# Causal attention over 23-step sequences: one sequence per 32 rows instead of four sequences in 92

## What is computed

```python
qk   = einsum('bthd,bshd->bhts', q, k) / sqrt(128)      # 8 heads of k and v, 2 of q on each, d = 128
gate = logG[:, :, :, None] - logG[:, :, None, :]         # logG: running sum over time of log_sigmoid(6.9 + x Wg)
a    = where(causal, qk ** 2 * exp(gate), 0)
norm = sum(a, axis=-1) + 1e-06
y    = einsum('bhts,bshd->bthd', a, v) / norm
out  = y @ Wc + bc
```

## Time and profile before

| | |
|---|---|
| median of 3 runs | 1438.3 us (1438.11 to 1441.32) |
| the profiled execution's own time | 1435.07 us |
| its span (first to last instruction) | 1433.3 us |
| TensorE busy | 1279.8 us, 89% of the span |
| VectorE busy | 915.9 us, 64% |
| ScalarE busy | 639.1 us, 45% |
| mean granted TensorE clock | 0.94 of 2.4 GHz |
| the first attention's loop | from about 140 us to about 651 us |

### The profile page before, as it was taken

The page is one execution under the profiler, slowest core; times in us unless marked ns, Lnnn a source line. Parts: engine busy times, 40 slices in busy tenths (PEclk is TensorE's granted clock), DMA queues, the critical chain, the costliest instruction groups (busy, mean ns, idle before and its releaser), DMA issues.

```text
span 1433.3 us, 28634 instructions
## 1 busy us (share of the span) xinstructions
PE 1279.8 (89%) x9689; PEld 789.5 (55%) x9690; DVE 915.9 (64%) x1920; ACT 639.1 (45%) x1086; POOL 231.4 (16%) x280
## 2 busy tenths in 40 slices
PE   6999999999999999996789999999986787859997
PEld 2447667677676767664435444544533565424443
DVE  5993665656656665668864555445348676778886
ACT  3444444554444445542325444444532433246664
POOL 2220000000000000000013333333347610110000
PEclk9997999999999999995799999999997787889999
DMA  5211452433435352422325867876336620000000
GB/s 191 73 66 62 161 199 104 182 135 143 182 141 199 123 191 103 176 89 83 141 75 200 280 220 246 318 256 208 109 121 137 100 36 2 1 0 16 22 22 26
DMA packets 42699, 184.21 MB, mean 129 GB/s; under 512 B 8688, under 2 KB 9200, under 8 KB 34832
## 3 DMA queue, kind: packets, MB, share of 16 engines
q0 software_dynamic: 19744, 95.41, 20.1%
q1 hardware_dynamic: 19440, 75.41, 14.8%
q10 hardware_dynamic: 3456, 12.58, 2.5%
HBM read 135.65 MB, written 47.73 MB: 128 GB/s over the span
## 4 chain that ended last, share of the span: by engine, by line
PE 58%; DVE 19%; issue 11%; DMA 4%; POOL 3%; ACT 2%; DVEq 1%; SPq 0%; ACTq 0%; POOLq 0%
PE ps L915 14%; PE ps L917 14%; PE ps L916 14%; PE ps L1021 3%; PE ps L1000 3%; DMA wide<-wsp 2%; DVE ff L2022 2%; DVE amf L2029 1%; PE ps L1105 1%; PE ps L1037 1%; POOL h L519 1%; PE ps L1358 1%; DVE bst L1460 1%; PE ps L1340 1%; DVE wa_lo L1387 1%
## 5 line engine op out<-in xcount | busy, mean ns | idle before, releaser
L915 PE MATMUL ps<-nT_hi,wa_hi 128*128 128x368 f16 x576 | 189.5, 329 | 11.1 <-DVE wa_lo L1387 8.1
L916 PE MATMUL ps<-nT_lo,wa_hi 128*128 128x368 f16 x576 | 189.1, 328 | 0.0
L917 PE MATMUL ps<-nT_hi,wa_lo 128*128 128x368 f16 x576 | 188.7, 328 | 0.0
L661 ACT ACTIVATE qk<-ps 128x368 f32<-128x368 f32 x128 | 60.4, 477 | 130.6 <-PE ps L917 130.5
L1751 DVE SCALAR_TENSOR_TENSOR nrm<-ps,xg,nrm 128x256 f32<-128x256 f32 x61 | 29.5, 484 | 123.8 <-ACT nrm L729 108.4
L915 PE MATMUL ps<-wide,xT 128*128 x244 | 92.7, 380 | 15.5 <-issue 12.3
L503 POOL DMA_INDIRECT xg<-xrow,idx x61 | 61.3, 1005 | 265.2 <-PE ps L1105 123.5
L1579 DVE TENSOR_TENSOR a<-sq,E 92x368 f32<-92x368 f32 x64 | 32.7, 538 | 107.1 <-ACT sq L677 107.1
L1553 DVE SCALAR_TENSOR_TENSOR wide<-ps,wide 128x368 f32<-128x368 f32 x128 | 69.3, 542 | 49.0 <-PE ps L917 49.0
L916 PE MATMUL ps<-wide,xT 128*128 x244 | 92.5, 379 | 0.0
L917 PE MATMUL ps<-wide,xT 128*128 x244 | 92.5, 379 | 0.0
(11 more groups left out here) (312 smaller groups left out, 3098.3 us busy)
## 6 DMA issues: line engine op xcount, KB each, us to landing
we_st<-in_we POOLq DMA_DIRECT2D x16, 1536.0 KB, 6.7
wsp<-we_sp POOLq DMA_DIRECT2D x16, 1536.0 KB, 5.3
wide<-wsp SPq DMA_DIRECT2D x16, 1536.0 KB, 7.6
yslot<-yt POOLq DMA_DIRECT2D x61, 256.0 KB, 4.3
wq_st<-in_ffq SPq DMA_DIRECT2D x24, 512.0 KB, 4.2
wq_st<-in_ffq ACTq DMA_DIRECT2D x24, 512.0 KB, 3.6
wide<-in_wa SPq DMA_DIRECT2D x10, 1024.0 KB, 6.1
xt<-in_x SPq DMA_DIRECT2D x12, 512.0 KB, 3.4
```

Source lines behind the costliest of these rows:

```text
L661: nc.scalar.activation(B["qk"][:, j, :], ps[:, j % 2, 0:CW], ACT.Copy, scale=(AS if j == 3 else 1.0) / WS).then_inc(b_ev, 1)
L915: nc.tensor.matmul(dst, lhs[0], rhs[0], start=start, stop=False)
L916: nc.tensor.matmul(dst, lhs[0], rhs[1], start=False, stop=False)
L917: return nc.tensor.matmul(dst, lhs[1], rhs[0], start=False, stop=stop)
```

## The change

In the first attention a sequence takes 32 rows (23 used), and four sequences stand side by side in the 128 rows. k and v are evicted into padded tiles `kp`, `vp` (16 sequences x 32 columns a chunk). The scores are 16 matmuls of 32 keys by 2 x 23 columns, each on its own 32 output partitions, and hold no products between sequences: 184 columns a chunk in place of 736. Gates and their exp have 92 columns in place of 368. The norm comes from a matmul with a block matrix of ones `blk` on the weights (one float32 matmul of 184 columns, signalled by `b_sm`), VectorE takes its reciprocal and scales the weights. The weights by values are 16 matmuls with v as the stationary side (32 rows, 128 columns) and 46 moving columns; their result is already turned, so L1037's transposes and the normalization behind them are gone. Row 23 of each 32 carries the 1e-6 (`eps_row`). `out_proj(g-1, c-1)` is placed in two halves around the sum's matmul, and `accumulate` of block 1 stands behind the scaling on VectorE. ScalarE's `unit_a_hi` moves ahead of the |w| sums in chunk 3. `gr` is read by four DMAs a head of 23 partitions x 368 values each; `lgd` is written in 92-byte pieces.

In the second attention `returned(3)`, `total_stats(3)` stand behind the first two `low`; `returned(5)`, `total_stats(5)`, `deviations` stand behind the first two rotations; the low halves of tiles 3 to 5 stand ahead of `centred(0)`; GpSimd's `turned_root(1)` stands ahead of a memset and three shares.

```diff
+        def windows(y, x):
+
+            return y[:].rearrange("p r t -> p (r t)").rearrange("p (n q s) -> p q n s", q=4, s=SL)[:, 2 * x:2 * x + 2]
+
+        def weighted(x):
+
+            return ps[:, 2 + 2 * x:4 + 2 * x, 0:REP * AT].rearrange("p q (n s) -> p q n s", s=SL)
...
-            sp.dma_start(B["gr"][0:AT], lgd[0:1, :].broadcast_to([AT, T])).then_inc(gr_in, 16)
-            sp.wait_ge(gr_in, 16)
+
+            def gates_spread(head):
+                for q in range(4):
+                    sp.dma_start(B["gr"][32 * q:32 * q + SL].rearrange("p a s -> p (a s)"),
+                                 lgd[q].rearrange("(h a) s -> h (a s)", h=HEADS)[head, :].broadcast_to([SL, AT * 4])).then_inc(gr_in, 16)
+
+            gates_spread(slice(0, 1))
+            sp.wait_ge(gr_in, 64)
...
             shares(2, 1)
+            turned_root(1)
             pool.wait_ge(wa_lo, UNITS)
             nc.gpsimd.memset(st_a[:], 0.0).then_inc(f_pad, 1)
             shares(2, 2)
-            turned_root(1)
             shares(2, 3)
...
-                nc.scalar.activation(B["qk"][:, j, :], ps[:, j % 2, 0:CW], ACT.Copy,
-                                     scale=(AS if j == 3 else 1.0) / WS).then_inc(b_ev, 1)
+                if j < REP:
+                    nc.scalar.activation(B["q"][:, j, :], ps[:, j % 2, 0:CW], ACT.Copy, scale=1.0 / WS).then_inc(b_ev, 1)
+                else:
+                    nc.scalar.activation(B["kp" if j == 2 else "vp"][:, :, 0:SL], ps[:, j % 2, 0:CW].rearrange("p (w s) -> p w s", s=SL),
+                                         ACT.Copy, scale=(AS if j == 3 else 1.0) / WS).then_inc(b_ev, 1)
 
...
                 for c in range(CH):
                     g = CH * i + c
                     for j in range(1 if c == 1 else 0, 4):
                         head_moved(g, c, j)
                     act.wait_ge(b_g, g + 1)
-                    nc.scalar.activation(B["E"][0:AT], B["gt"][0:AT], ACT.Exp).then_inc(b_E, 1)
-                    for j in range(2):
-                        act.wait_ge(b_sc, 3 * g + j + 1)
-                        nc.scalar.activation(B["sq"][0:AT, j].rearrange("p a r t -> p (a r t)"), ps[0:AT, 2 + j, 0:2 * REP * AT],
-                                             ACT.Square, scale=float(DH) ** -0.5).then_inc(b_sq, 1)
-                    act.wait_ge(b_sc, 3 * g + 3)
-                    nc.scalar.activation(B["v1"][0:AT, :, 0:DH],
-                                         ps[0:AT, 1, :].rearrange("p (a b) -> p a b", a=4), ACT.Copy).then_inc(b_ev, 1)
+                    nc.scalar.activation(B["E"][:], B["gt"][:].rearrange("p a s -> p (a s)"), ACT.Exp).then_inc(b_E, 1)
+                    act.wait_ge(b_sc, 2 * g + 1)
+                    nc.scalar.activation(B["sq"][:].rearrange("p r x -> p (r x)"), ps[:, 2, REP * AT:2 * REP * AT],
+                                         ACT.Square, scale=float(DH) ** -0.5).then_inc(b_sq, 1)
+                    act.wait_ge(b_sc, 2 * g + 2)
+                    nc.scalar.activation(B["v1"][:].rearrange("p a d -> p (a d)"), ps[:, 1, :], ACT.Copy).then_inc(b_ev, 1)
+                    if c == CH - 1:
+                        unit_a_hi(i + 1, b_pj, 4 * CH * (i + 1))
...
                     if c in (1, 3):
                         expert_hi(2 * i + c // 2)
                     if c == 0:
                         head_moved(g + 1, 1, 0)
-                    for j in range(2):
-                        act.wait_ge(b_yt, 2 * g + j + 1)
-                        nc.scalar.activation(oh[:, :, j * 2 * AT:(j + 1) * 2 * AT],
-                                             ps[:, 2 + j, 0:CW].rearrange("p (r t) -> p r t", r=REP), ACT.Copy).then_inc(b_hi, 1)
+                    act.wait_ge(b_av, g + 1)
+                    for x in range(2):
+                        nc.scalar.activation(windows(B["yT_hi"], x), weighted(x), ACT.Copy).then_inc(b_hi, 1)
...
-                        pe.wait_ge(b_lo, free(2 * g + j))
-                        for a in range(2):
-                            tok = slice((2 * j + a) * AT, (2 * j + a + 1) * AT)
-                            ins = nc.tensor.matmul(ps[0:AT, 2 + j, a * REP * AT:(a + 1) * REP * AT],
-                                                   B["qk"][:, 2, tok], B["qk"][:, 0:2, tok], start=True, stop=True)
-                        ins.then_inc(b_sc, 1)
+                    pe.wait_ge(b_lo, free(2 * g + 1))
+                    for a in range(4):
+                        for q in range(4):
+                            n = 4 * a + q
+                            out = ps[32 * q:32 * q + 32, 2, REP * AT:2 * REP * AT].rearrange("p (r a s) -> p r a s", r=REP, a=4)
+                            ins = nc.tensor.matmul(out[:, :, a, :], B["kp"][:, n, :], B["q"][:, :, n * SL:(n + 1) * SL],
+                                                   start=True, stop=True)
+                    ins.then_inc(b_sc, 1)
 
                     pe.wait_ge(b_ev, ready(5 * g + 3))
                     for a in range(4):
-                        ins = nc.tensor.transpose(ps[0:AT, 1, a * P:(a + 1) * P], B["qk"][:, 3, a * AT:(a + 1) * AT], ident[:])
+                        ins = nc.tensor.transpose(ps[:, 1, a * P:(a + 1) * P],
+                                                  B["vp"][:, 4 * a:4 * a + 4, :].rearrange("p w s -> p (w s)"), ident[:])
                     ins.then_inc(b_sc, 1)
                     if c == 0:
                         head_project(g + 1, 1, 0)
                     else:
                         if c == 1:
                             pe.wait_ge(wb_lo, i + 1)
-                        out_proj(g - 1, c - 1)
-                    pe.wait_ge(b_ev, ready(5 * g + 4))
-                    for j in range(2):
-                        pe.wait_ge(b_a, 2 * g + j + 1)
-                        if j == 1:
-                            pe.wait_ge(b_acc, 4 * g + 2)
-                        for a in range(2):
-                            for r in range(REP):
-                                ins = nc.tensor.matmul(ps[0:AT, 4 + 2 * j + a, r * (DH + 1):(r + 1) * (DH + 1)],
-                                                       B["a"][0:AT, j, a, r, :], B["v1"][0:AT, 2 * j + a, :],
-                                                       start=True, stop=True)
-                        ins.then_inc(b_av, 1)
-
+                        out_proj(g - 1, c - 1, (0, 1))
+                    pe.wait_ge(b_a, 2 * g + 1)
+                    nc.tensor.matmul(ps[:, 3, REP * AT:2 * REP * AT], B["blk"][:], B["a"][:].rearrange("p r x -> p (r x)"),
+                                     start=True, stop=True).then_inc(b_sm, 1)
                     if c == 0:
                         head_project(g + 1, 1, 1)
-                    elif c < CH - 1:
+                    else:
+                        out_proj(g - 1, c - 1, (2, 3))
+                    pe.wait_ge(b_ev, ready(5 * g + 4))
+                    pe.wait_ge(b_a, 2 * g + 2)
+                    for a in range(4):
+                        for q in range(4):
+                            w = slice(32 * q, 32 * q + 32)
+                            ins = nc.tensor.matmul(ps[:, 2 + q, 0:REP * AT].rearrange("p (r a s) -> p r a s", r=REP, a=4)[:, :, a, :],
+                                                   B["v1"][w, a, :], B["a"][w, :, a * SL:(a + 1) * SL], start=True, stop=True)
+                    ins.then_inc(b_av, 1)
+
+                    if 0 < c < CH - 1:
                         head_project(g + 1, c + 1, 0)
-                    elif not last:
+                    elif c == CH - 1 and not last:
                         pe.wait_ge(wa_lo, i + 2)
                         head_project(g + 1, 0, 0)
-                    for j in range(2):
-                        pe.wait_ge(b_yn, 2 * g + j + 1)
-                        for r in range(REP):
-                            for a in range(2):
-                                ins = nc.tensor.transpose(ps[:, 2 + j, (2 * r + a) * AT:(2 * r + a + 1) * AT],
-                                                          B["yn"][0:AT, j, a, r, :], ident[0:AT, 0:AT])
-                        ins.then_inc(b_yt, 1)
                 if not last:
                     head_project(g + 1, 0, 1)
...
+                order.enter(i, 1 + CH * 2 + 1)
+                order(V.tensor_copy(B["LGh"][:], B["LG"][:, ds(i, 1), :].rearrange("p a b -> p (a b)")))
                 for c in range(CH):
                     g = CH * i + c
                     if c == 0:
-                        dve.wait_ge(gr_in, 16 * (i + 1))
+                        dve.wait_ge(gr_in, 64 * (i + 1))
                         dve.sem_inc(passed, 1)
-                    order(V.tensor_tensor(B["gt"][0:AT], B["gr"][0:AT, c * CW:(c + 1) * CW].rearrange("p (a t) -> p a t", a=4),
-                                          B["LGh"][0:AT, 4 * c:4 * c + 4].unsqueeze(2).broadcast_to([AT, 4, AT]), ALU.subtract))
+                    order(V.tensor_tensor(B["gt"][:], B["gr"][:, 4 * c:4 * c + 4, :],
```

(74 more changed lines are left out.)

63 lines of the change are left out of this document (29 added, 34 removed).

## The result

The changed kernel takes **1430.0 us** (median of 20 runs, 1420.7 to 1436.7); the kernel before takes 1437.4 us beside it (20 runs, 1434.1 to 1448.2): ratio 0.9942, 95% interval 0.9922 to 0.9961. The profiled execution took 1430.10 us (span 1428.3), 5.0 less than the profiled one of before.

The account below looks back on a forecast made before the run. TensorE's distances between starts bound the first attention, with VectorE entering the chain after the change. Terms -14.4 - 4.7 + 6 - 0.5 = -13.6 us; 1438.3 - 13.6 = 1424.7 us, 8 in 10 range 1409 to 1443.

Parts of the forecast that it names:

- The wait: Block 3 of out_proj waits for VectorE's accumulation of block 1, behind reciprocal and scaling: 1.68 us, 24 times, 40 us.
- the tiles' gain: First attention's new tiled scores and products on TensorE, taken alone: -1.4 us a chunk, -45 us over 32 chunks.
- The tiles' prices: First attention, per chunk: scores and v's transposes 1.3 us, products with v 1.1 us, reciprocal 1.30 us, scaling 0.35 us.
- price of an entry: TensorE switching into tiled matmuls in the first attention costs about 0.1 us; leaving them costs about 0.2 us.
- The sum over a head: First attention's four chunks: -1.21, +0.28, +0.28, -1.15 us, so -1.8 us a head, -14.4 us over eight heads.
- The clock: About every fourth new stall in front of block 3 followed by half clock: six of 24, +6 us, ends 0 and 38.
- clock falls at most stalls: Rival at block 3's wait: 1.6 us each, outweighs the gain from 12 of 24; at 16, 1444 us; chance 0.12.
- The loop's start: Four gate reads land in 3 us before the first attention's loop, so TensorE does not wait: -4.7 us, at worst 0.
- The second attention: Reordered work there: first projection 0.4 us sooner, root 8 us sooner, scores 2.8 us later; -0.5 us, ends -3 and +3.
- the rival of 5 us: Second attention's new order costs 5 us and more through a longer stretch at half clock: 1430 us; chance 0.06.
- the prediction's own signs: First attention: no 3 us gap at the loop's start; wrong if a head takes under 60 or over 64 us.

Follow-up runs that it names:

- Experiment 1: Changed kernel with VectorE accumulating block 1 of out_proj before it waits for the sum: 1389.2 us, ratio 0.9661 to the kernel before.
- experiment 2: Changed kernel with the reciprocal of the sums computed twice in a row on VectorE: 1516.2 us, ratio 1.0564 to the kernel before.
- experiment 3: Changed kernel with 18 unused matmuls between blocks 2 and 3 of out_proj, filling TensorE's wait: 1418.6 us, ratio 0.9868 to the kernel before.
- Experiment 4: Changed kernel with each gate read of 23 rows split into 16 and 7: 1417.5 us, repeated 1420.6 us.
- Experiment 6: Changed kernel with block 1 accumulated early, gate reads split, chunk 3's yT low half earlier: 1384.2 us; with the second attention's old order also 1384.8 us.

## Why the prediction was right or wrong

**The wait: right, in its place, its count and nearly its size.** With T the start of the sum's matmul, block 3 was to start at T+2.92 and the next float16 work at T+4.96; they start at T+2.82 and T+4.89 (227.30 and 229.37 less 224.48). Without the wait it is T+1.24 in the forecast; the stall is 1.58 us, 24 times, where 1.68 was said. Experiment 1 removes it, and experiment 2 lengthens it by the 1.35 us that VectorE's chain got longer. That nearly all of the tiles' gain is given back at once holds.

**The tiles' prices: right.** The blocks were taken from the earlier trace rows. Scores and transposes take 1.13 us from the first score to the next float16 start, with the entry of 0.10 ahead of it 1.23 us against 1.3; products with v from 228.34 to 229.37, 1.03 + 0.10 against 1.1; the reciprocal 1.307 against 1.30; the scaling 0.350 against 0.35. The Trainium skill ("TensorEngine Tiling (Array Packing)", Key Properties) has a change of the tiling mode drain the engine. Here the trace agrees as far as it goes: from the last matmul of block 3 to the first product it is 228.34 - 228.09 = 0.25 us, 0.10 more than the usual 0.156 between starts, and that is the prediction's price of an entry.

**The sum over a head: right in sign, its gain 0.7 us too small.** Undisturbed chunks against before: chunk 0 -1.23 (said: -1.21), chunks 1 and 2 +0.02 and +0.17 (+0.28 each), chunk 3 -1.50 (-1.15). VectorE's queue as the longest way of chunk 3 was right: in an undisturbed one the sum's matmul starts at 255.44 (block 3 at 258.26) and its own out_proj at 264.60, T+9.16 where T+9.2 was said. Of the 0.74 us that a head is off, 0.35 are in chunk 3, most of it in the kernel before, whose own way there was added up too short: a wait of 0.46 us in front of L1037 was not in it. The rest is in chunks 1 and 2, where scores and transposes came out 0.07 us shorter and the products ended 0.07 sooner than said, and in chunk 1 the kernel before is 0.15 longer than its sum. Over the loop this is -19.1 us, where 14.4 was said.

The wait in the kernel before, and then chunk 3 of the changed one:

```profile
198.61 0.54 PE L1037 MATMUL ps<-ident,yn 92*128 92x92 f32 x4 [0.46 <-DVE yn L1595]
```

```profile
255.44 0.47 PE L1038 MATMUL ps<-a,blk 128*128 128x184 f32 x2
...
258.26 0.33 PE L935 MATMUL ps<-yT_hi,wb_hi 128*128 128x368 f16 x1 [1.41 <-DVE wide L1579]
...
263.49 0.98 DVE L1626 TENSOR_TENSOR yT_lo<-ps,yT_hi 128x368 f16<-128x368 f32 x2
...
264.60 0.33 PE L935 MATMUL ps<-yT_hi,wb_hi 128*128 128x368 f16 x1
```

**The clock: the mechanism right, the size half of what it is.** The step was "Six of 24: +6 us", 1.6 us a stall with a third of it hidden in waits on VectorE. There are nine, and the price of 1.6 us was right but for the hiding: they cost 1.64 us in chunks 1 and 2, where nothing hides them, since the stretch lies behind the wait and not in it, and 1.2 in chunk 3. That is +13.4 in the trace, 11.4 by experiment 3. With it the rival "clock falls at most stalls" comes nearer than its 0.12 suggests: nine is three short of the 12 of 24 from which it put no gain at all.

**The loop's start: wrong.** "Four reads of 34 KB [...] should land in 3 us", for -4.7 us. They land in 6.44, the write takes 2.67 in place of 1.70, and TensorE idles 3.54 us in place of 3.01: +0.2. The reads of 23 rows ran with a DMA share of 0.06, one of 16 engines; the old read of 92 rows had 0.22, about four of them. Stretches with the columns of the earlier trace rows, DMA share and GB/s last; the kernel before, while it reads the gates:

```profile
137.00:143.00 6.00, 6.00 (x42) 4.43 (x40) 0.00 (x0) 0.95 (x2) 0.00 (x0) 1.00 0.22 90
```

and the changed kernel, while it reads them:

```profile
139.00:145.30 6.30, 4.49 (x58) 2.67 (x56) 0.00 (x0) 0.61 (x2) 0.00 (x0) 1.00 0.06 21
```

The estimate counted bytes and took it for granted that they spread over engines. Experiment 4 takes 3.0 us off the landing by rows of 16 alone. The Trainium skill says why ("DMA: Bandwidth & Descriptors", "Why a DMA increments its semaphore by 16 and not by 1"): a transfer is dealt to as many engines, at most 16, as divide its slowest dimension on both sides. 23 is prime and leaves one, 92 leaves four; the two shares agree with it. The forecast did not weigh this.

**The second attention: right, at nothing.** Counted from the loop's end, the first projection starts 0.6 us sooner (said: 0.4), the root is computed 6.9 us sooner (8), the scores start 1.7 later (2.8), and the wait of 2.70 us in front of the next transposes is gone:

```profile
1085.93 0.47 PE L935 MATMUL ps<-nT_hi,wa_hi 128*128 128x368 f16 x1 [4.18 <-DVE nT_lo L1442]
...
1105.38 6.57 PE L1264 MATMUL ps<-kr,qp 32*128 32x23 f32 x128 [2.90 <-DVE qp L1905]
1111.87 1.97 PE L930 MATMUL ps<-ident,nrm 128*128 128x128 f32 x8
1114.49 1.09 PE L930 MATMUL ps<-ident,nrm 128*128 128x128 f32 x4 [0.65 <-DVE nT_lo L1442]
1117.09 0.46 PE L935 MATMUL ps<-nT_hi,wa_hi 128*128 128x368 f16 x1 [1.50 <-DVE nT_lo L1442]
```

What TensorE waits for here is VectorE now, and the end is where it was. Experiment 6 puts the order at 0 within the scatter of its runs, 1 us in the traces, and the rival of 5 us is out.

In all: -19 for -14.4, +0.2 for -4.7, +13 for +6, 0 for -0.5. Two errors, of about 7 and 5 us, made the kernel slower than said, and one of 5 us made it faster. That the time lies 5.3 us from the forecast is in part luck, since these cancel in part; the wait and its cause are not. Two of the prediction's own signs went against it: two heads take 64.34 us and the first 70.71, over the 64 that it allowed, and the gap of over 3 us at the loop's start is still there.

## What to carry to other kernels

Look at what stands between a wait and the next release on the same in-order engine. VectorE waited for the sums with a finished block behind it in its program, and TensorE needed that block's bank: one instruction placed ahead of the wait, where VectorE had nothing to do, was worth 41 us, more than five times what the cheaper matmuls brought without it.

When a stream of matmuls gets a new wait, price the clock after it as well as the wait. Here a wait of 1.41 us cost 1.2 to 1.6 us more at nine of 24 places, and at least 19 of 24 waits of 2.75 us were followed by such a stretch.

For a small transfer on the path, look at how its rows divide as well as at its bytes: rows of 16 and 7 landed 3.0 us sooner than rows of 23.

## What the runs showed of the hardware that was not expected

- Waits of 1.15 us at the end of each head did not bring the clock down in the kernel before (none of seven); waits of 1.10 us at the same place did in one or two of seven in the kernels of experiments 1 and 6, which have the tile blocks ahead of them. 14 matmuls of no use in each took the last falls away and 4.2 us off the median. The profiled executions differ by 5.4 us: 1.33 are the one fall, 0.8 lie in the first head, and 3.3 behind the loop, where the two programs are the same; so not all of the gain can be put down to the filling.
- 432 matmuls of no use made the kernel 11 us faster.
- Eight DMAs issued one after the other take 0.28 to 0.42 us each on SyncE; with eight reads the issues (137.79 to 140.60) are the larger part of the 4.4 us, and the DMA behind the last only 1.58.
- The stretch from the loop's end to the end of the kernel took 776 to 782 us in kernels that do the same there (776.3, 778.7, 779.6, 781.8, 782.1), with the stretches at 1.2 GHz in different places; why was not tried.
